# Two reciprocal square roots of a convolution kernel computed as a power on GpSimd

## The reference, cut to what matters

```
def _gn(v, G=32, eps=1e-05):                     # pairs of channels of one image
    m = mean(g); s = var(g)
    return (g - m) / sqrt(s + eps)

def _L0_conv_ref(x, w_off, gamma, beta, w_pw):
    offsets = conv3x3(pad(x), w_off)
    xd = bilinear_sample(pad(x), grid + offsets)
    mean, var = mean(xd), var(xd)                # per channel, over images and pixels
    xn = (xd - mean) * rsqrt(var + EPS) * gamma + beta
    return einsum(relu(xn), w_pw)

x = x + _L0_conv_ref(_gn(x), ...)
x = x + _L1_conv_ref(_gn(x), ...)
```

## Time and profile before

| what | value |
|---|---|
| median of 3 runs | 124.84 us |
| lowest to highest | 123.85 to 124.96 us |
| span of the profiled execution | 123.2 us |
| PE busy | 93.8 us, 76% |
| DVE busy | 92.9 us, 75% |
| ACT busy | 59.3 us, 48% |
| POOL busy | 9.9 us, 8% |
| chain that ended last | PE 64%, DVE 14%, DMA 6%, ACT 6% |

### The profile page before, as it was taken

How to read it: one execution, slowest core, us unless ns; L and a number is a source line. 1 busy time by engine, 2 the same in 40 slices (tenths; PEclk the granted TensorE clock), 3 DMA queues, 4 the chain that set the end, 5 groups by cost and what they waited for, 6 DMA issues and landing times.

```text
span 123.2 us, 1759 instructions
## 1 busy us (share of the span) xinstructions
PE 93.8 (76%) x601; PEld 71.9 (58%) x601; DVE 92.9 (75%) x273; ACT 59.3 (48%) x98; POOL 9.9 (8%) x22
## 2 busy tenths in 40 slices
PE   0999999999999999925930029999999989896000
PEld 0886767666666676603710029999677978674000
DVE  6487559399999999999999999656759955552700
ACT  3059794967869666493059000007343355341600
POOL 7007200000000005000001601000000000000000
PEclk9999999999999999995596555699999999998555
DMA  3550687807869472893000040000000000000085
GB/s 103 173 205 7 136 183 226 228 10 180 226 203 246 88 212 23 185 278 97 0 0 3 2 128 0 0 0 0 8 0 0 0 0 5 0 0 0 0 206 177
DMA packets 6392, 10.90 MB, mean 88 GB/s; under 512 B 1648, under 2 KB 3440, under 8 KB 6384
## 3 DMA queue, kind: packets, MB, share of 16 engines
q1 hardware_dynamic: 5824, 8.93, 26.8%
q0 software_dynamic: 400, 1.58, 5.5%
q10 hardware_dynamic: 160, 0.30, 0.7%
HBM read 3.10 MB, written 5.14 MB: 67 GB/s over the span
## 4 chain that ended last, share of the span: by engine, by line
PE 64%; DVE 14%; DMA 6%; ACT 6%; issue 3%; POOL 1%; DVEq 0%; POOLq 0%
PE ps L604 20%; PE ps L568 11%; PE ps L611 11%; PE ps L712 5%; PE ps L683 5%; DMA slot_map<-gmap_scratch,gather_rows 3%; PE ps L646 3%; DMA x_pairs<-in_x_dram 3%; PE ps L585 2%; PE ps L669 2%; DVE result L937 2%; DVE rows_at_x L857 2%; ACT rows_at_x L453 1%; PE ps L654 1%; ACT positive_offsets L468 1%
## 5 line engine op out<-in xcount | busy, mean ns | idle before, releaser
L604 PE MATMUL ps<-gmap,w_off_taps 128*128 128x336 f32 (+1 forms) x96 | 28.8, 450 | 0.0
L568 PE MATMUL ps<-ident 128*128 128x128 f32 x104 | 16.4, 327 | 13.6 <-DMA slot_map<-gmap_scratch,gather_rows 10.6
L604 PEld LDWEIGHTS ps<-gmap,w_off_taps 128*128 128x128 f32 x96 | 18.1, 195 | 10.7 <-issue 4.3
L568 PEld LDWEIGHTS ps<-ident 128*128 128x128 f32 x104 | 15.7, 239 | 14.1 <-issue 11.0
L611 PE MATMUL ps<-gmap,w_off_taps 64*128 64x288 f32 (+1 forms) x96 | 15.9, 443 | 0.0
L611 PEld LDWEIGHTS ps<-gmap,w_off_taps 64*128 64x128 f32 x96 | 11.0, 185 | 3.4 <-issue 2.7
L629 PE MATMUL ps<-x_halves,ident 128*128 128x288 f32 x16 | 7.0, 594 | 4.0 <-DMA x_halves<-in_x_dram 4.0
L459 ACT COPY offsets<-ps 64x576 f32<-64x576 f32 x8 | 5.0, 630 | 9.3 <-PE ps L611 9.3
L857 DVE COPY_PREDICATED rows_at_x<-positive_offsets,x_differences 128x864 f32<-128x864 int32 x8 | 9.0, 1129 | 0.0
L872 DVE TENSOR_TENSOR rows_at_x<-rows_at_x,hmap 128x864 f32<-128x864 f32 x8 | 8.4, 1051 | 0.0
L864 DVE TENSOR_TENSOR rows_at_x<-rows_at_x,offsets 128x864 f32<-128x864 f32 x8 | 8.4, 1050 | 0.0
(11 more groups left out here) (175 smaller groups left out, 149.1 us busy)
## 6 DMA issues: line engine op xcount, KB each, us to landing
offset_scratch<-offsets SPq DMA_DIRECT2D x8, 288.0 KB, 2.6
gmap_scratch<-gmap SPq DMA_DIRECT2D x8, 196.0 KB, 3.0
gmap<-gmap SPq DMA_DIRECT2D x7, 189.0 KB, 2.6
hmap<-gmap SPq DMA_DIRECT2D x12, 98.0 KB, 2.5
x_pairs<-in_x_dram SPq DMA_DIRECT2D x4, 288.0 KB, 3.3
x_halves<-in_x_dram POOLq DMA_DIRECT2D x2, 576.0 KB, 7.4
out_dram<-result SPq DMA_DIRECT2D x2, 360.0 KB, 4.2
out_dram<-result SPq DMA_DIRECT2D x2, 216.0 KB, 3.1
```

Of the source, the lines that this page charges most:

```text
L568: mm(ps[:, bank, 0:P], ident[:], ident[:], start=True, stop=True)
L604: mm(psf[:, par, col:col + PC * (m1 - m0)], wt[:, kx, :], conv_window(gmap[:, b], kx + 2 + 2 * GR * m0, m1 - m0), start=(kx == 0), stop=False)
```

## The change

The first group norm tile and the batch norm no longer take ACT's square root and DVE's reciprocal. DVE adds epsilon to the variance by itself (in the group norm through the deviation's product, in the batch norm through the new `vareps`), and GpSimd raises the sum to the power of -0.5 with one `tensor_tensor` of one element a partition, against a constant tile `minushalf`. The first of these stands between GpSimd's memsets and its iotas, the second at the end of its program, behind the branch. Tiles 1 to 3 of the group norm and all later square roots stay on ACT.

```
--- before.py
+++ after.py
@@ -88,6 +88,8 @@
         id15 = sb("ident_times_1_5", [P, C])
         eps = sb("eps", [P, 1])
         neg1 = sb("minus_one", [P, 1])
+        minushalf = sb("minus_half", [P, 1])
+        vareps = sb("bn_var_and_eps", [P, 1])
         iotaq = sb("position", [P, B, Q])
         iotag = sb("map_coordinate", [P, GR])
         f_row0 = sb("offset_row_base", [P, 1])
@@ -109,6 +111,7 @@
         xd = sb("sampled", [P, B, Q])
         top8 = sb("top8", [P, 8])
         at8 = sb("at8", [P, 8], u32)
+        bnrstd = sb("bn_rstd", [P, 1])
         slmean = sb("slot_value_over_n", [P, 1])
         bnt = sb("bn_slot_term", [P, 1])
         zero = sb("zero", [P, 1])
@@ -381,6 +384,8 @@
             nc.gpsimd.memset(windows(gmap[:, :, 3 * GR - 2:3 * GR + 2], H - 1, GR), 0.0).then_inc(maps_zero, 1)
             nc.gpsimd.memset(hmap[:, 0:2, 0:MR:MR - 1, :], 0.0).then_inc(maps_zero, 1)
             nc.gpsimd.memset(hmap[:, 0:2, 1:MR - 1, 0:MC:MC - 1], 0.0).then_inc(maps_zero, 1)
+            pool.wait_ge(gn1_v, 1)
+            nc.gpsimd.tensor_tensor(r1[:, 0:1], v1[:, 0:1], minushalf[:], ALU.pow).then_inc(gn1_sd, 1)
             whole = dict(allow_small_or_imprecise_dtypes=True)
             steps.link(nc.gpsimd.iota(iotaq[:], [[1, B * Q]], base=0, channel_multiplier=0, **whole))
             steps.link(nc.gpsimd.iota(iotag[:], [[1, GR]], base=-1, channel_multiplier=0, **whole))
@@ -418,6 +423,8 @@
                 rounds = nc.gpsimd.value_load(mosti[0:1, :])
                 with nc.gpsimd.Fori(0, rounds) as n:
                     gather(n + 2)
+            pool.wait_ge(bn_v, 1)
+            nc.gpsimd.tensor_tensor(bnrstd[:], bnv[:, 0:1], minushalf[:], ALU.pow).then_inc(bn_sd, 1)
 
         @block.scalar
         def _(act):
@@ -470,7 +477,6 @@
                     act.wait_ge(across, 3 * (b - 2) + 3)
                 nc.scalar.activation(ab[:, par], kq, ACT.Abs).then_inc(abs_ok, 1)
 
-            gn1_std(1, 0, 1)
             act.wait_ge(gn1_ok, 1)
             fill_gmap(0)
             act.wait_ge(wtrans, 2)
@@ -502,8 +508,6 @@
             act.wait_ge(excess_ok, 1)
             nc.scalar.activation(xr[:], xr[:], ACT.Sign, accum_out=count[:]).then_inc(count_ok, 1)
 
-            act.wait_ge(bn_v, 1)
-            nc.scalar.activation(bnv[:, 0:1], bnv[:, 0:1], ACT.Sqrt, bias=eps[:]).then_inc(bn_sd, 1)
             act.wait_ge(bn_ok, 1)
             for b in range(0, B, 2):
                 act.wait_ge(slot_put, b // G2 + 1)
@@ -756,6 +760,7 @@
                 last = v.memset(lane[:, j:j + 1], float(j))
             then(last)
             v.memset(eps[:], EPS)
+            v.memset(minushalf[:], -0.5)
             then(v.memset(ident[:], 0.0))
             wait()
             link(v.transpose(lanet[:], lane[:]))
@@ -803,6 +808,17 @@
                     last = v.bn_aggr(mv1[:, t, :], st1[:, t].rearrange("p a n -> p (a n)"))
                 last.then_inc(gn1_mv, 1)
 
+            def gn1_first_scale():
+
+                dve.wait_ge(gn1_ps, 1)
+                view = pstat[:, 0:2]
+                link(v.scalar_tensor_tensor(dev1[:, 0:1], view[:, 0:1], -0.5, mv1[:, 0, 0:1], ALU.mult, ALU.add))
+                link(v.scalar_tensor_tensor(dev1[:, 0:1], dev1[:, 0:1], dev1[:, 0:1], eps[:], ALU.mult, ALU.add))
+                v.scalar_tensor_tensor(v1[:, 0:1], view[:, 1:2], 0.5, dev1[:, 0:1], ALU.mult, ALU.add).then_inc(gn1_v, 1)
+                dve.wait_ge(gn1_sd, 1)
+                v.scalar_tensor_tensor(nb1[:, 0:1], view[:, 0:1], -0.5, r1[:, 0:1], ALU.mult,
+                                       ALU.mult).then_inc(gn1_ok, 1)
+
             def gn1_scale(g, t0, t1):
                 dve.wait_ge(gn1_ps, g)
                 view = pstat[:, 0:2 * T].rearrange("p (t k) -> p t k", t=T)[:, t0:t1, :]
@@ -816,7 +832,7 @@
                                        ALU.mult).then_inc(gn1_ok, 1)
 
             gn1_mean_var(0, 1)
-            gn1_scale(1, 0, 1)
+            gn1_first_scale()
             dve.wait_ge(maps_zero, 5)
             dve.wait_ge(gn1_ok, 1)
             v.tensor_scalar(interior(0, C, 1, 2), xp_[0:C, 0, :].rearrange("p (r k) -> p r k", k=W), r1[0:C, 0:1],
@@ -971,9 +987,10 @@
 
 
             link(v.bn_aggr(mv2[:], st2[:].rearrange("p a n -> p (a n)")))
+            v.tensor_scalar(vareps[:], mv2[:, 1:2], EPS, None, ALU.add)
             link(v.tensor_scalar(bnt[:], mv2[:, 0:1], -2.0, None, ALU.mult))
             link(v.scalar_tensor_tensor(bnt[:], slmean[:], float(B * Q - 1), bnt[:], ALU.mult, ALU.add))
-            v.scalar_tensor_tensor(mv2[:, 1:2], bnt[:], slmean[:], mv2[:, 1:2], ALU.mult, ALU.add)
+            v.scalar_tensor_tensor(mv2[:, 1:2], bnt[:], slmean[:], vareps[:], ALU.mult, ALU.add)
             v.tensor_tensor(mv2[:, 0:1], mv2[:, 0:1], slmean[:], ALU.add).then_inc(bn_mv, 1)
 
             def put_slot(b0, b1):
@@ -988,8 +1005,7 @@
             v.scalar_tensor_tensor(bnv[:, 0:1], g2[:, 1, 0:1], g2[:, 1, 0:1], g2[:, 0, 1:2], ALU.mult,
                                    ALU.add).then_inc(bn_v, 1)
             dve.wait_ge(bn_sd, 1)
-            link(v.reciprocal(bnv[:, 1:2], bnv[:, 0:1]))
-            link(v.tensor_tensor(bnv[:, 1:2], bnv[:, 1:2], gb[:, 0:1], ALU.mult))
+            link(v.tensor_tensor(bnv[:, 1:2], bnrstd[:], gb[:, 0:1], ALU.mult))
             link(v.scalar_tensor_tensor(bnv[:, 2:3], g2[:, 0, 0:1], -1.0, bnv[:, 1:2], ALU.mult, ALU.mult))
             v.tensor_tensor(bnv[:, 3:4], bnv[:, 2:3], gb[:, 1:2], ALU.add).then_inc(bn_ok, 1)
             put_slot(G2, B)
```

## The result

| | before | after |
|---|---|---|
| median | 124.66 us | 128.93 us |
| lowest to highest, 4 runs each | 123.85 to 124.96 | 128.12 to 129.23 |
| span of the profiled execution | 123.2 us | 127.2 us |
| PE busy | 93.8 us | 94.5 us |
| POOL busy | 9.9 us | 11.1 us |

The ratio of after to before is 1.034 with a 95% interval of 1.027 to 1.041: slower by 4.3 us. The forecast was 129.7. The number came close; the first link of the reasoning under it was false, and two others were too small. Medians are of all executions, while a ratio leaves out, as slow ones, those over 1.5% above the quickest of the same kernel, so that it can differ from the quotient of the medians.

A forecast was written before the change was run, and what follows sets the result against it. The chain through the first convolution was taken as the bound, PE holding 64% of it. Terms 3.3 + 1.4 + 0 + 0.2 = 4.9 on 124.84 gave 129.7 us, own range 127.9 to 131.6.

The forecast's parts named there:

- the first link of the reasoning: First group norm: first power waits behind POOL's library reload, starts at 9.95, so tile 0's shift comes 3.3 us later.
- The same 3.3 for the first convolution: Start: the shift's 3.3 us delay passes through the weights' copy to the first convolution, from 8.57 to 11.9.
- TensorE after the pause: First convolution: PE's 3.3 us idle stretch brings slower products on restart, +1.4 us, range 0 to 1.9.
- The second table load: ACT behind L453: reloading the square root's set, 1.28 us, ends at 18.0 before the root is due at 18.5; cost 0.
- The second power's time of start: Batch norm: power behind the reload after the all-reduce, ready at 84.4 to 84.9; L992 1.4 to 1.9 us late.
- The second power's price: Batch norm: L992's delay of 1.4 to 1.9 us less 1.5 hidden behind PE's work, +0.2 us, ends 0 and 0.9.
- lateness and cover: Batch norm: L992 1.4 to 1.9 us late, against 1.5 us from first relu piece (84.71) to PE being ready (86.27).
- Rival 2: Both powers: they need no library, the first starts at 6.46, the reload is free; 124.6 us, chance 0.06.
- Rival 1: Both powers: library loads only when the power is dispatched, first at 13.45, second at 89.28; 138.8 us, chance 0.30.

## Why the prediction was right in its number and wrong in its steps

**The same 3.3 for the first convolution: wrong, 1.48 measured, and from something else.** The prediction moved the iotas by 0.3 and looked only at when their results are wanted. It didn't look at what would run beside them. Before, the long iota came after the copy; now it comes with it, and the copy takes 2.03 for 0.57. This holds in the first power alone too, where 3.60 for the power, 1.47 for the copy and 1.52 for PE's slower records (6.01 less 4.49) make 6.59, the delay of its second convolution (21.62, before 15.03), which in the times is 6.7 us by the medians and 6.2 by the ratio. The Trainium skill has the rule that I passed over (SBUF — State Buffer, section "SBUF: two separate sides"): DVE and GpSimd share a pair of ports as an exclusive lock, so that a DVE instruction which uses both ports for one tensor waits for the whole GpSimd instruction ahead of it, while one with two inputs from SBUF is at odds only with a GpSimd instruction that reads SBUF. The runs here agree, in both halves: 2.03 and 2.04 for the one-tensor copy, 0.81 for the two-tensor form beside an iota, which only writes.

**TensorE after the pause, +1.4, range 0 to 1.9: right in kind, 1.96 measured.** A pause of 1.60 cost more than one of 3.3 was expected to, just above the range, and more than the 5.26 of the first power alone did (1.52). The size doesn't follow the pause's length in these two. The start of 4.49 from which it was counted is itself one of two: 3.44 in another execution.

**The second table load, 0: right.** It is over at 15.36, the square root starts at 17.25 for want of its variance.

**The second power's time of start: right.** By the steps of the prediction (register load 0.85, reload 6.50 to 7.02 behind the all-reduce's end at 80.43) it would be 87.8 to 88.3; it was 87.94. The power takes 0.59 and not 0.3, and the next DVE step was 1.8 late beyond the general shift (5.23 less 3.42), inside the 1.4 to 1.9.

**The second power's price, +0.2, ends 0 and 0.9: wrong, mis-sized, 1.0 by the two profiles, 1.5 to 2.1 by the ratios.** The term was a difference of two numbers of like size, lateness and cover, and the cover came from one execution. The 52 records ahead of it took between 7.63 and 8.91 in the twelve profiles; each of them shifts the cover by the difference. In the kernel after they took 0.63 less than before: with that, 1.8 of lateness less 1.5 of cover become 0.9, nearly all of the 1.00 that PE waited.

**The sum.** 4.9 was forecast, 4.3 measured. 3.3 for a reload that wasn't there stands against 1.5 for a blocked copy, 0.6 more for TensorE's slow phase and 0.8 (by the two profiles, 1.00 less 0.2) to 1.9 (by the ratios, 2.1 less 0.2) more for the second power. The errors cancelled, and that the number came close was luck. Rival 2 was right about the start of the first power (6.41; 6.46 was its number) for a wrong reason: the power does need the library. Rival 1 fell. The prediction had named two signs of being wrong: that the first convolution moves by other than 3.1 to 4.0 us, or that PE waits long for `relu_out`. It moved by 1.48, and PE waited 1.00.

**What stays open.** Half a per cent between the second power alone (1.3%) and both powers with the iota ahead (1.8%). The intervals overlap, and without the all-reduce the two are equal (1.001 both). The profiles have a lead and no more: POOL stood 8.30 us between all-reduce and power with the iota ahead and 7.80 with the second power alone, but over all profiles such waits run from 7.52 to 8.36. Whether the late iota without a power costs less than in the kernel after isn't settled, given how far its times lie apart; a shorter pause would be a reason, and that wasn't tested by itself. The lower clock level in the first convolution of the kernel after is read from the pace of its records, since the column of the clock doesn't show it. What the second reload would cost without the one ahead of the all-reduce is an estimate. A power on DVE instead of GpSimd wasn't tried.

## What to carry to other kernels

Ask of a GpSimd library reload which library the program holds when it gets there, the last one of the program counting as the first of the next execution: adding or removing one instruction at the end can move 7 us at the start. Two reloads in a row, out to another library and back, can put an instruction behind both of them. When an edit moves a long GpSimd instruction, look at which DVE instructions it will now run beside, and in which form they are. A cost that is hidden behind a cover of like size needs the cover from several executions, above all where TensorE restarts ahead of it.

## What the runs showed of the hardware

- **GpSimd's power of one element a partition takes 0.56 to 0.59 us**, four times its small iotas (0.12 to 0.14), and about what ACT's square root and DVE's reciprocal took together (0.53, from start of the one to start of the shift).
